# TensorE's order in an attention unit: eight value instructions as one block, both mask matmuls behind it

## The chip, the cores and the metric

The kernel runs on one core of a Trainium2 chip. Its time is the device time in microseconds (us) of one launch. PE is TensorE's matmul row in the profile and PEld its weight loads, DVE is VectorE, ACT is ScalarE, POOL is GpSimd, and SP is the engine that issues the DMAs.

## The reference, cut to what matters

32 batches of x with 256 rows and 128 columns pass an attention of 16 heads of width 64 and then a feed-forward part whose operands are quantized to FP4. The part of the attention that this change is about:

```python
s = jnp.einsum('bhid,bhjd->bhij', q * scale, k)
gm = jax.lax.stop_gradient(jnp.max(s, axis=-1, keepdims=True))
causal_mask = jnp.triu(jnp.ones((N, N), bool), 1)
p = jnp.where(causal_mask, 0.0, jnp.exp(s - gm))
num = jnp.einsum('bhij,bhjd->bhid', p, v)
out = num / (jnp.sum(p, axis=-1, keepdims=True) + EPS)
out = out.transpose(0, 2, 1, 3).reshape(B, N, H * Dh)
return out @ Wo + bo
```

The maximum `gm` is taken over all scores, the masked ones too. So the kernel must read the whole bank for the maximum first, and may put the mask on it only after that.

## The kernel before, in words

A batch is cut into eight units (0 to 7) of two heads each. The engines run the same loop over the batches, each with its own order written out by hand, and semaphores tie them together. The attention of a unit is a pipeline over several units. In unit u, TensorE does in this order:

- the first place, (u, "a"): always a `qk` step, the projection of q and k of the unit two further on into one of two PSUM banks `ps_m` (L825, three matmuls on `wq_r`, three on `wkv_r`);
- the scores of head 0 (L908, four matmuls into `ps_s`);
- the second place, (u, "b"): a step of another part, such as `gate` (units 1 and 2), `wo` (unit 3, the output projection of the batch before, L863) or `v`;
- the scores of head 1 (L908). They go to a bank that both units use, so they wait for the exponentials of unit u-1 (`exp_done`);
- the transposes of the probabilities of unit u-2 (L804, `ps_t`);
- the third place, (u, "c"): `v` in units 0 and 3, `up` in 1 and 2, `xt` in 4, `hqt` in 5, `down` in 6, none in 7;
- `mask(u, 0)` (L917, one bf16 matmul that adds a large negative number to the diagonal blocks of head 0's bank);
- the value product of unit u-3 (L960, 64 output columns for each head): two instructions for the first 128 keys, then `mask(u, 1)`, then two for the last 128 keys. The profile shows each of these fp32 instructions as two records, eight in all for a unit.

The steps in the places take the two `ps_m` banks in turn, and each first waits until the step before it in its bank has been read. In units 0 to 5 the third place has the bank that the first place of the same unit filled. So it waits for `qk_ready`, which DVE signals when it has subtracted the rounded part (L664), and DVE can do that only behind ACT's cast (L547).

ACT's order in a unit: the cast of the first place's `qk` (L547), its reads for the second place, the copies of the transposes (L570, L572), its reads for the third place, four exponentials (L583: two for each head; each head waits for its own mask through `masked`), and the copy of the value product out of PSUM (L590, which signals `ot_ready`). DVE's order: the maximum of head 0 (L774), the subtraction L664, the maximum of head 1, the reciprocals of the sums (L788, L791), and then its other parts. POOL multiplies the probabilities by the reciprocals (L454, L456) and rounds for the FP4 parts. `wo` in unit 3 waits for `ot_ready` of the last unit of its batch, which ACT signals at the end of unit 2.

Of the kernel before, what the change touches and what calls it, by code (L numbers as in the profile page):

```python
# [13 lines left out]
P = 128  # L14
# [70 lines left out]
def adaln_block(nc, x, w_q, w_kv, w_o, b_o, w_gate, w_up, w_down, cond, w_mod, out):  # L85
# [14 lines left out]
    with ExitStack() as ctx:  # L100
# [95 lines left out]
        def scores_bank(u, h):  # L196

            return u % 2 if h == 0 else 2
# [101 lines left out]
        def i_is(i, n):  # L300

            return isinstance(i, int) and i == n

        def iterations(eng, body, last=B - 1):

            for i in range(-1, 3):
                body(i)
            with eng.Fori(3, last) as i:
                body(i)
            for i in range(last, B + 2):  # L310
                body(i)
# [17 lines left out]
        def shared_steps(i):  # L329

            steps = []
            for at in ([i - 1] if not isinstance(i, int) or i > -1 else []) + [i]:
                for n, place in enumerate(sorted(PLACES)):
                    kind, behind, part = PLACES[place]
                    if i_is(at, 1) and place in WEIGHT_PLACES:
                        steps.append((at is i, place, "weights", 0, WEIGHT_PLACES.index(place), n % 2))
                    elif not isinstance(at, int) or 0 <= at - behind < B:
                        steps.append((at is i, place, kind, at - behind, part, n % 2))
            found = {}
            for n, (now, place, kind, b, part, bank) in enumerate(steps):  # L340
                if now:
                    same = [x for x in steps[:n] if x[5] == bank]
                    found[place] = (kind, b, part, bank, same[-1][2:5] if same else None)
            return found
# [457 lines left out]
        def _(pe):  # L802
            def transpose(dst, src, n=P):
                return nc.tensor.transpose(dst, src, ident[0:n, 0:n])  # L804
# [87 lines left out]
            def body(i):  # L892
                has = Has(i)
                shared = shared_steps(i)

                def at_place(u, place):
                    if (u, place) in shared:
                        kind, b, k, bank, before = shared[u, place]
                        if before is not None:

                            ready, per_batch = READ[before[0]]
                            pe.wait_ge(ready, per_batch * before[1] + (before[2] + 1) * per_batch // PARTS[before[0]])
                        shared_step(kind, b, k, bank)

                def scores(u, h):
                    for t in range(2):
                        for part in range(2):
                            mm = nc.tensor.matmul(ps_s[:, scores_bank(u, h), t * N:(t + 1) * N],  # L908
                                                  stack[:, u % 4, h, 0, t * P:(t + 1) * P], stack[:, u % 4, h, 2 - part, :],
                                                  start=(t == 0 and part == 0), stop=(part == 1), skip_group_check=True)  # L910
                    mm.then_inc(s_full, 1)

                def mask(u, h):

                    pe.wait_ge(max_ready, 16 * i + 2 * u + h + 1)
                    diagonals = ps_s[:, scores_bank(u, h), :].rearrange("p (n j) -> p n j", j=P)[:, 0:4:3, :]
                    nc.tensor.matmul(diagonals, ident_b[:, :], later_b[:, :].unsqueeze(1).to_broadcast([P, 2, P]),  # L917
                                     start=False, stop=True, skip_group_check=True).then_inc(masked, 1)

                for u in range(UNITS):  # L920
                    par = u % 2
                    at_place(u, "a")

                    if has.attn:
                        pe.wait_ge(stacked[par], STACKED * i + UNIT_STACKED * (u // 2 + 1))
                        scores(u, 0)
                    at_place(u, "b")
                    if has.attn:
                        if has.after(u - 1):
                            pe.wait_ge(exp_done, 16 * i + 2 * (u - 1) + 2)  # L930
                        scores(u, 1)
                    if i_is(i, 0) and u == 2:
                        pe.wait_ge(setup_dve, SETUP_ROWS)
                    if has.unit(u - 2):

                        g = (u - 2) % UNITS
                        for h in range(2):
                            pe.wait_ge(probs_ready, 16 * i + 2 * (u - 2) + h + 1)
                            if has.after(u - 3):
                                pe.wait_ge(pt1_ready if h else pt0_ready, UNITS * i + u - 2)  # L940
                            for c in range(3):
                                mm = transpose(ps_t[:, h, c * P:(c + 1) * P], probs[:, g % 4, h, c * P:(c + 1) * P])
                            mm.then_inc(pt_full, 1)
                    at_place(u, "c")
                    if has.attn:
                        mask(u, 0)
                    if has.unit(u - 3):

                        w = (u - 3) % UNITS
                        pe.wait_ge(pt0_ready, UNITS * i + u - 2)  # L950
                        pe.wait_ge(pt1_ready, UNITS * i + u - 2)
                        if u >= 3:
                            pe.wait_ge(v_ready, 4 * i + (4 if w >= UNITS // 2 else 2))
                        if has.after(u - 4):
                            pe.wait_ge(ot_ready, UNITS * i + u - 3)
                    for n, (keys, q0) in enumerate(((0, 0), (1, P))):
                        if has.unit(u - 3):
                            for h in range(2):
                                head = (2 * w + h) * DH
                                mm = nc.tensor.matmul(ps_o[h * DH:(h + 1) * DH, q0:N], v[:, keys, head:head + DH],  # L960
                                                      probs_t[:, w % 2, h, (0 if n == 0 else N):(N if n == 0 else 3 * P)],
                                                      start=(n == 0), stop=(n == 1), skip_group_check=True)
                        if n == 0 and has.attn:
                            mask(u, 1)
                    if has.unit(u - 3):
                        mm.then_inc(o_full, 1)

            iterations(pe, body)


# [19 lines left out]
```

## Time and profile before

| what | before |
|---|---|
| median of 3 runs | 1419.08 us (1416.86 to 1421.19) |
| span of the profiled execution | 1416.3 us |
| granted TensorE clock, mean | 0.981 of full speed |
| PE, DVE, ACT, POOL busy | 96%, 81%, 68%, 61% |
| chain that ended last | PE 46%, POOL 27%, issue 13%, DVE 9% |
| mask L917, PE | 512 matmuls, 143.6 us |
| value product L960, PE | 2048 records, 278.8 us |

The profiled execution took 1416.3 us from its first to its last instruction, 2.8 us under the median of the runs. PE's busy time overlaps itself, since its matmuls are pipelined and their ends are modelled. So lengths on PE are best read from the start of one group to the start of the next. A row of the timeline stands for a group of the same instructions in a row, with its start, its length and the count.

### The profile page before, as it was taken

To read this page: it belongs to the slowest core of one execution; us is meant where nothing else is said; L and a number is where in the kernel's file an instruction comes from. 1 tells how busy PE (TensorE), PEld (TensorE's weight loads), DVE (VectorE), ACT (ScalarE), POOL (GpSimd) and SP (SyncE) were. 2 spreads that over 40 slices of the span, in tenths; PEclk is the share of its full clock that TensorE was granted. 3 is DMA by queue.
4 is the path that set the end of the run, shared out by engine and by line. 5 is a ranking of instruction groups with operands and counts; after the bars stand their busy time and mean duration, and the time that the engine had idled before them with its cause. 6 is when DMAs were issued, how large, how long until landed. Compare 5 with 4: busy or idle time off the path is not lost.

```text
span 1416.3 us, 37184 instructions
## 1 busy us (share of the span) xinstructions
PE 1361.8 (96%) x10194; PEld 1077.6 (76%) x10194; DVE 1146.0 (81%) x2821; ACT 964.8 (68%) x3269; POOL 868.4 (61%) x1582
## 2 busy tenths in 40 slices
PE   4899999999999999999999999999999999999993
PEld 3677787778777787877778777777877787787772
DVE  5668888888888888888888888888888888888774
ACT  2767667667767667767767767766776767676750
POOL 0556666766666666656666566666666666665663
PEclk6999999999999999999999999999999999999995
DMA  5766777767677676677767667776667776667740
GB/s 153 184 164 161 163 173 175 170 161 162 161 169 179 165 166 162 160 169 177 167 165 164 159 161 176 174 167 161 162 161 169 179 167 164 162 161 169 167 97 10
DMA packets 160941, 227.99 MB, mean 161 GB/s; under 512 B 27376, under 2 KB 90736, under 8 KB 160912
## 3 DMA queue, kind: packets, MB, share of 16 engines
q1 hardware_dynamic: 160912, 227.65, 68.3%
q8 instruction: 13, 0.21, 0.1%
q14 instruction: 16, 0.13, 0.0%
HBM read 21.94 MB, written 4.28 MB: 19 GB/s over the span
## 4 chain that ended last, share of the span: by engine, by line
PE 46%; POOL 27%; issue 13%; DVE 9%; SPq 2%; DMA 1%; POOLq 1%; ACT 1%; DVEq 0%; ACTq 0%
PE ps_m L825 15%; POOL probs L456 10%; PE ps_o L960 9%; PE ps_s L908 8%; PE ps_t L804 6%; POOL qy L74 4%; POOL qy L72 4%; POOL hq L76 3%; PE ps_m L888 3%; PE ps_s L917 3%; DVE neg_max L774 2%; POOL rstd L464 1%; POOL h L492 1%; POOL h2a L488 1%; POOL probs L454 1%
## 5 line engine op out<-in xcount | busy, mean ns | idle before, releaser
L774 DVE TENSOR_REDUCE neg_max<-ps_s 128x2 f32<-128x512 f32 x512 | 351.4, 687 | 170.6 <-PE ps_s L908 165.2
L583 ACT ACTIVATE probs<-ps_s,neg_max 128x128 f32<-128x128 f32 (+1 forms) x1024 | 419.2, 427 | 39.5 <-PE ps_s L917 36.4
L456 POOL TENSOR_SCALAR probs<-probs,r_den 128x256 f32<-128x256 f32 (+1 forms) x768 | 380.3, 511 | 0.0
L454 POOL TENSOR_TENSOR probs<-probs,r_den 128x128 f32<-128x128 f32 x256 | 102.7, 401 | 427.0 <-DVE r_den L791 422.2
L908 PE MATMUL ps_s<-stack 128*128 128x256 f32 x2048 | 329.6, 287 | 3.5 <-DMA stack<-qk_parts 3.2
L908 PEld LDWEIGHTS ps_s<-stack 128*128 128x128 f32 x2048 | 285.3, 190 | 10.9 <-DMA stack<-qk_parts 4.4
L960 PE MATMUL ps_o<-probs_t,v 128*64 128x256 f32 (+1 forms) x2048 | 278.8, 351 | 0.0
L804 PE MATMUL ps_t<-ident,probs 128*128 128x128 f32 x1536 | 220.2, 275 | 4.1 <-POOL probs L456 0.4
L583 ACT ACTIVATION_READ_ACCUMULATOR probs<-ps_s,neg_max 128x1 f32 x1024 | 216.3, 211 | 0.0
L570 ACT COPY probs_t<-ps_t 128x384 f32<-128x384 f32 x160 | 77.0, 481 | 192.1 <-PE ps_t L804 192.1
L804 PEld LDWEIGHTS ps_t<-ident,probs 128*128 128x128 f32 x1536 | 172.8, 140 | 16.2 <-POOL probs L456 11.9
L664 DVE TENSOR_TENSOR qk_parts<-ps_m,qk_parts 128x512 fp32r<-128x512 f32 x256 | 174.2, 680 | 4.9 <-ACT qk_parts L547 4.9
L572 ACT COPY probs_t<-ps_t 128x384 f32<-128x384 f32 x256 | 123.8, 483 | 76.6 <-PE ps_t L804 76.5
L547 ACT CAST qk_parts<-ps_m 128x512 fp32r<-128x512 f32 x256 | 154.7, 604 | 17.4 <-PE ps_m L825 5.4
L825 PE MATMUL ps_m<-h_r,wq_r 128*128 128x256 f32 x768 | 159.6, 316 | 5.1 <-DVE h_r L599 1.6
L960 PEld LDWEIGHTS ps_o<-probs_t,v 128*64 128x64 f32 x2048 | 101.5, 134 | 73.5 <-issue 27.6
L825 PEld LDWEIGHTS ps_m<-h_r,wq_r 128*128 128x128 f32 x768 | 107.9, 190 | 50.8 <-issue 45.3
L917 PE MATMUL ps_s<-later_b,ident_b 128*128 128x256 bf16 x512 | 143.6, 281 | 2.5 <-DVE neg_max L774 2.2
L917 PEld LDWEIGHTS ps_s<-later_b,ident_b 128*128 128x128 bf16 x512 | 49.2, 96 | 126.6 <-issue 93.7
L825 PE MATMUL ps_m<-h_r,wkv_r 128*128 128x256 f32 x768 | 135.2, 285 | 0.0
L825 PE MATMUL ps_m<-wkv_r,h_r 128*128 128x512 f32 x384 | 117.6, 415 | 5.1 <-DVE qk_parts L664 4.2
L863 PE MATMUL ps_m<-wo,o_t 128*128 128x128 f32 x1024 | 119.5, 275 | 0.6 <-DVE hh L688 0.6
(109 smaller groups left out, 2018.4 us busy)
## 6 DMA issues: line engine op xcount, KB each, us to landing
stack<-qk_parts SPq DMA_DIRECT2D x512, 192.0 KB, 2.7
stack<-qk_parts SPq DMA_DIRECT2D x512, 128.0 KB, 2.7
stack<-qk_parts SPq DMA_DIRECT2D x512, 64.0 KB, 2.3
mod_a<-mod_rows SPq DMA_DIRECT2D x32, 256.0 KB, 4.0
x_in<-L_attn_x SPq DMA_DIRECT2D x32, 128.0 KB, 2.1
x_res<-L_attn_x SPq DMA_DIRECT2D x32, 128.0 KB, 2.1
out<-y_out SPq DMA_DIRECT2D x32, 128.0 KB, 1.9
mod_b<-mod_rows SPq DMA_DIRECT2D x32, 64.0 KB, 2.8
```

Source lines behind the costliest of these rows:

```text
L456: ins = nc.gpsimd.tensor_scalar(cols, cols, r_den[:, par, s:s + 1], 1.0, ALU.mult, ALU.mult)
L547: nc.scalar.copy(qk_parts[:, k % 2, :, 0, :], ps_m[bank][:, :].rearrange("p (n j) -> p n j", n=2)).then_inc(qk_high, 1)
L572: nc.scalar.copy(probs_t[:, u % 2, 1, :], ps_t[:, 1, 0:3 * P]).then_inc(pt1_ready, 1)
L583: ins = nc.scalar.activation(probs[:, u % 4, h, t * P:(1 + 2 * t) * P], ps_s[:, scores_bank(u, h), t * N:t * N + (1 + t) * P], ACT.Exp, bi ...
L664: nc.vector.tensor_tensor(qk_parts[:, k % 2, :, 1, :], ps_m[bank][:, :].rearrange("p (n j) -> p n j", n=2), qk_parts[:, k % 2, :, 0, :], A ...
L774: nc.vector.tensor_reduce(neg_max[:, par, 2 * h:2 * h + 2], ps_s[:, scores_bank(u, h), :].rearrange("p (t j) -> p t j", t=2), AX.X, ALU.ma ...
L804: return nc.tensor.transpose(dst, src, ident[0:n, 0:n])
L825: mm = nc.tensor.matmul(dst, left[l], right[r], start=(n == 0), stop=(n == 2))
L863: mm = nc.tensor.matmul(ps_m[bank][:, t * P:(t + 1) * P], o_t[:, u, t * P:(t + 1) * P], wo[:, u, :], start=(u == 0), stop=(u == UNITS - 1))
L908: mm = nc.tensor.matmul(ps_s[:, scores_bank(u, h), t * N:(t + 1) * N], stack[:, u % 4, h, 0, t * P:(t + 1) * P], stack[:, u % 4, h, 2 - pa ...
L917: nc.tensor.matmul(diagonals, ident_b[:, :], later_b[:, :].unsqueeze(1).to_broadcast([P, 2, P]), start=False, stop=True, skip_group_check= ...
L960: mm = nc.tensor.matmul(ps_o[h * DH:(h + 1) * DH, q0:N], v[:, keys, head:head + DH], probs_t[:, w % 2, h, (0 if n == 0 else N):(N if n == ...
```

## The change

Only TensorE's program changes. The value product of unit u-3 is issued as one block of four instructions (eight records) right behind the third place, and both masks of unit u follow the block.

```diff
                     at_place(u, "c")
-                    if has.attn:
-                        mask(u, 0)
                     if has.unit(u - 3):
...
-                    for n, (keys, q0) in enumerate(((0, 0), (1, P))):
-                        if has.unit(u - 3):
+                        for n, (keys, q0) in enumerate(((0, 0), (1, P))):
                             for h in range(2):
...
-                        if n == 0 and has.attn:
-                            mask(u, 1)
-                    if has.unit(u - 3):
                         mm.then_inc(o_full, 1)
+                    if has.attn:
+                        mask(u, 0)
+                        mask(u, 1)
```

The value product's line number becomes L957. The programs of ACT and DVE are the same, and so are those of POOL and SP, which the diff does not touch.

The first place is TensorE's row in unit 1 of a batch in the middle of the run, from the third place (`up`) to the first place of unit 2. Before:

```order
L825 MATMUL ps_m<-wgu_r,xq_r 128x352 [waits qk_ready]
L825 MATMUL ps_m<-wgu_r,xq_r 128x352 x2
L915 REGISTER_ALU
L917 MATMUL ps_s<-later_b,ident_b 128x2x128 [waits max_ready]
L960 MATMUL ps_o<-probs_t,v 64x256 [waits ot_ready,pt1_ready,pt0_ready]
L960 MATMUL ps_o<-probs_t,v 64x256
L915 REGISTER_ALU
L917 MATMUL ps_s<-later_b,ident_b 128x2x128 [waits max_ready]
L960 MATMUL ps_o<-probs_t,v 64x128 x2
L902 REGISTER_ALU
L825 MATMUL ps_m<-h_r,wq_r 128x256 [waits gated]
```

And now:

```order
L825 MATMUL ps_m<-wgu_r,xq_r 128x352 [waits qk_ready]
L825 MATMUL ps_m<-wgu_r,xq_r 128x352 x2
L957 MATMUL ps_o<-probs_t,v 64x256 [waits ot_ready,pt1_ready,pt0_ready]
L957 MATMUL ps_o<-probs_t,v 64x256
L957 MATMUL ps_o<-probs_t,v 64x128 x2
L915 REGISTER_ALU
L917 MATMUL ps_s<-later_b,ident_b 128x2x128 [waits max_ready]
L915 REGISTER_ALU
L917 MATMUL ps_s<-later_b,ident_b 128x2x128 [waits max_ready]
L902 REGISTER_ALU
L825 MATMUL ps_m<-h_r,wq_r 128x256 [waits gated]
```

The first mask has moved behind four value instructions, and the second follows it at once; the value instructions for the first and the last keys stand together.

The second place is TensorE's row from the end of unit 2 to the output projection `wo` in unit 3. Before:

```order
L960 MATMUL ps_o<-probs_t,v 64x256
L915 REGISTER_ALU
L917 MATMUL ps_s<-later_b,ident_b 128x2x128 [waits max_ready]
L960 MATMUL ps_o<-probs_t,v 64x128 x2
L825 MATMUL ps_m<-h_r,wq_r 128x256 [waits gated]
L825 MATMUL ps_m<-h_r,wq_r 128x256 x2
L825 MATMUL ps_m<-h_r,wkv_r 128x256 x3
L908 MATMUL ps_s<-stack 128x256 [waits stacked1]
L908 MATMUL ps_s<-stack 128x256 x3
L863 MATMUL ps_m<-wo,o_t 128x128 [waits ot_ready,h_ready]
L863 MATMUL ps_m<-wo,o_t 128x128 x15
L908 MATMUL ps_s<-stack 128x256 [waits exp_done]
```

And now:

```order
L915 REGISTER_ALU
L917 MATMUL ps_s<-later_b,ident_b 128x2x128 [waits max_ready]
L915 REGISTER_ALU
L917 MATMUL ps_s<-later_b,ident_b 128x2x128 [waits max_ready]
L825 MATMUL ps_m<-h_r,wq_r 128x256 [waits gated]
L825 MATMUL ps_m<-h_r,wq_r 128x256 x2
L825 MATMUL ps_m<-h_r,wkv_r 128x256 x3
L908 MATMUL ps_s<-stack 128x256 [waits stacked1]
L908 MATMUL ps_s<-stack 128x256 x3
L863 MATMUL ps_m<-wo,o_t 128x128 [waits ot_ready,h_ready]
L863 MATMUL ps_m<-wo,o_t 128x128 x15
L908 MATMUL ps_s<-stack 128x256 [waits exp_done]
```

The last mask of unit 2 now stands directly ahead of the `qk` step, with no value instructions between them; between the masks and the `wo` step, which waits for `ot_ready`, stand that step and four score matmuls, as before. (`REGISTER_ALU` rows compute the thresholds of waits.)

## Rows read from the trace of the kernel before

**Rows 1.** The page, busy time of each engine (us, share of the span, instructions)
```profile
PE 1361.8 (96%) x10194; PEld 1077.6 (76%) x10194; DVE 1146.0 (81%) x2821; ACT 964.8 (68%) x3269; POOL 868.4 (61%) x1582
```
**Rows 2.** The page, engines' shares of the chain that ended last
```profile
PE 46%; POOL 27%; issue 13%; DVE 9%; SPq 2%; DMA 1%; POOLq 1%; ACT 1%; DVEq 0%; ACTq 0%
```
**Rows 3.** Timeline of PE, one batch: start us, length us, engine, line, operation, xcount
```profile
699.77 0.97 PE L825 MATMUL ps_m<-wkv_r,h_r 128*128 128x512 f32 x3
700.58 0.28 PE L917 MATMUL ps_s<-later_b,ident_b 128*128 128x256 bf16 x1
...
704.80 0.75 PE L825 MATMUL ps_m<-wgu_r,xq_r 128*128 128x352 f32 x3
705.39 0.28 PE L917 MATMUL ps_s<-later_b,ident_b 128*128 128x256 bf16 x1
705.61 0.65 PE L960 MATMUL ps_o<-probs_t,v 128*64 128x256 f32 x4
...
706.77 0.61 PE L825 MATMUL ps_m<-h_r,wq_r 128*128 128x256 f32 x3
...
711.57 0.61 PE L825 MATMUL ps_m<-h_r,wq_r 128*128 128x256 f32 x3
...
712.86 3.73 PE L863 MATMUL ps_m<-wo,o_t 128*128 128x128 f32 x32
...
717.49 0.95 PE L825 MATMUL ps_m<-wkv_r,h_r 128*128 128x512 f32 x3
...
722.77 0.38 PE L804 MATMUL ps_m<-ident,xn 128*128 128x128 f32 x2
722.99 0.27 PE L917 MATMUL ps_s<-later_b,ident_b 128*128 128x256 bf16 x1
...
727.25 0.50 PE L804 MATMUL ps_m<-ident,hq 128*128 128x128 f32 x3
727.59 0.27 PE L917 MATMUL ps_s<-later_b,ident_b 128*128 128x256 bf16 x1
...
731.82 1.50 PE L888 MATMUL ps_m<-wd_t,hq_t 128*128 128x128 f32 x12
733.16 0.27 PE L917 MATMUL ps_s<-later_b,ident_b 128*128 128x256 bf16 x1
...
734.53 0.61 PE L825 MATMUL ps_m<-h_r,wq_r 128*128 128x256 f32 x3
...
737.66 0.27 PE L917 MATMUL ps_s<-later_b,ident_b 128*128 128x256 bf16 x1
...
741.86 0.97 PE L825 MATMUL ps_m<-wkv_r,h_r 128*128 128x512 f32 x3
```
**Rows 4.** Timeline of ACT in the same batch; in brackets the idle time before it
```profile
701.26 0.37 ACT L583 ACTIVATE probs<-ps_s,neg_max 128x128 f32<-128x128 f32 x1
...
702.86 0.39 ACT L590 COPY o_t<-ps_o 128x256 f32<-128x256 f32 x1
703.11 0.63 ACT L547 CAST qk_parts<-ps_m 128x512 fp32r<-128x512 f32 x1
...
733.47 0.37 ACT L583 ACTIVATE probs<-ps_s,neg_max 128x128 f32<-128x128 f32 x1 [0.97 <-PE ps_s L917]
```
**Rows 5.** Timeline of DVE in unit 1 of that batch
```profile
703.46 0.69 DVE L774 TENSOR_REDUCE neg_max<-ps_s 128x2 f32<-128x512 f32 x1 [1.16 <-PE ps_s L908]
704.07 0.68 DVE L664 TENSOR_TENSOR qk_parts<-ps_m,qk_parts 128x512 fp32r<-128x512 f32 x1
```
**Rows 6.** Timeline near the start, ACT and DVE, where the subtraction waits for the cast
```profile
22.08 0.59 ACT L547 CAST qk_parts<-ps_m 128x512 fp32r<-128x512 f32 x1 [2.53 <-PE ps_m L825]
...
22.70 0.69 DVE L664 TENSOR_TENSOR qk_parts<-ps_m,qk_parts 128x512 fp32r<-128x512 f32 x1 [2.36 <-ACT qk_parts L547]
```
**Rows 7.** Timeline of PE near the end: all value instructions of a unit, no mask
```profile
1372.73 0.87 PE L960 MATMUL ps_o<-probs_t,v 128*64 128x256 f32 x8
1373.53 1.23 PE L825 MATMUL ps_m<-wgu_r,xq_r 128*128 128x352 f32 x6
```

## The prediction

> **What bounds the kernel now.** I read three things in this order. First the page's busy times: PE is at 96% of the span, DVE at 81%, ACT at 68% [rows 1]. The chain that ended last is PE for only 46%, and POOL has 27% of it [rows 2], so PE's 96% isn't a proof that PE sets the time. Second, PE's timeline over one batch in steady state, because only the start-to-start distances show what PE can issue: from the third place of unit 0 to the same place of the next batch it takes 741.86 - 699.77 = 42.09 us [rows 3], and 32 batches of that are 1347 of the 1416 us. PE's rows hardly leave a gap. Third, and this decides, the timelines of ACT and DVE beside it: what does each third place on PE wait for, and with how much to spare?
>
> In unit 1 the third place starts at 704.80 [rows 3]. It waits for DVE's subtraction, which started at 704.07 [rows 5], so the way from the start of the subtraction to the place is 0.73 us. The subtraction started behind the maximum of head 0 (703.46, 0.69 long) and not behind ACT's cast, which ended at 703.11 + 0.63 = 703.74 [rows 4, 5]. So ACT's cast is early by about 0.3 us. What sets the cast is ACT's own row: four exponentials from 701.26, the copy of the value product at 702.86, the cast at 703.11 [rows 4]. That row cannot start before mask 0.
>
> This gives a loop that closes in every unit whose third place waits for the subtraction: first exponential E, cast, subtraction, third place, mask 0, next E. Now mask 0 comes directly behind the third place, and the loop has slack. The change puts the whole value block into it.
>
> **What the change takes off PE.** Before, from the first mask to the next first place: 706.77 - 705.39 = 1.38 us [rows 3]. The same eight value records without a mask among them take 1373.53 - 1372.73 = 0.80 [rows 7]. A mask takes 705.61 - 705.39 = 0.22 ahead of value instructions; three 512-column matmuls take 700.58 - 699.77 = 0.81, at most 0.135 for each 256 columns [rows 3], so some 0.09 of the 0.22 is the passage to the 64-column instructions. My estimate for the new stretch: 0.09 to get into the block, 0.80 for it, 0.11 for each mask = 1.11, which is 0.27 less than 1.38. Bounds: the passage costs 0 to 0.10; the block costs 0.80 to 0.95 (the latter is 1.38 less two masks of 0.22, as if the two halves saved nothing together). If PE alone set the time, this would be 256 units x 0.27 = 69 us of gain.
>
> The Trainium skill, "TensorEngine Tiling (Array Packing)", section Key Properties, says that changing the tiling mode, not just the tile, drains the engine. The rows agree as far as they go: the 0.22 against 0.135, and 0.80 against 0.95. By that rule the change has two mode changes a unit where before had four, and one of the two now stands ahead of E.
>
> **What it adds to the loop.** E now comes at the third place's own length T, plus 0.09, plus 0.80, plus the way from mask 0 to the exponential where ACT is free, 733.47 - 733.16 = 0.31 [rows 3, 4]. Together T + 1.20. From E on: four exponentials 702.86 - 701.26 = 1.60; the copy 703.11 - 702.86 = 0.25 [rows 4]; cast to subtraction 22.70 - 22.08 = 0.62 where DVE really waited for it [rows 6], which I take as 0.66 because that cast was 0.59 long and the one behind the copy is 0.63; subtraction to third place 0.73. Sum 3.24. The loop is then 4.44 + T. Nothing hides it: ACT's row and DVE's subtraction are in series with PE. The maximum of head 0, now early, doesn't bind any more.
>
> Now unit by unit, E to E [all T from rows 3]:
> - unit 0 (`v`): T = 0.81, so 5.25.
> - units 1 and 2 (`up`): T = 705.39 - 704.80 = 0.59, so 5.03 each, 10.06.
> - unit 3: here PE has more than 4 us of `wo`, so the loop over the subtraction is loose. But `wo` waits for the copy of the last unit's value product, on ACT behind the exponentials of unit 2. The copy ends at E + 1.60 + 0.39 = 1.99 [rows 4]; with 0.06 for the semaphore (a subtraction's end at 704.07 + 0.68 lies 0.05 ahead of the place that waits for it) `wo` starts at 2.05. PE would be there sooner: masks end 0.09 before E (0.22 less 0.31), and from the first place to `wo` it is 712.86 - 711.57 = 1.29, so at 1.20. The 0.85 us that PE had ahead are lost in front of `wo`. From `wo` to the third place 717.49 - 712.86 = 4.63, then 0.81 (a `v`) + 1.20: 8.69.
> - unit 4 (`xt`): T = 722.99 - 722.77 = 0.22, so 4.66. Unit 5 (`hqt`): T = 727.59 - 727.25 = 0.34, so 4.78.
> - unit 6 (`down`): its third place is not tied to its own first place; it comes 731.82 - 727.25 = 4.57 behind that of unit 5, held by DVE and POOL work that starts with unit 5's subtraction. I keep that. T = 733.16 - 731.82 = 1.34. E to E: 4.57 + 1.34 - 0.34 = 5.57.
> - unit 7 (no third place): PE alone. From the first place to mask 0 737.66 - 734.53 = 3.13, plus 1.20, less 0.09: 4.24.
>
> Sum: 5.25 + 10.06 + 8.69 + 4.66 + 4.78 + 5.57 + 4.24 = 43.25 us a batch against 42.09, so 1.16 more; x 32 = 37 us. The profiled execution would go from 1416.3 to about 1453, and the median, which stands 2.8 us above it, from 1419.1 to **1456 us**, 2.6% slower.
>
> Edits with little effect: both masks wait for maxima that DVE has done by then (head 1's maximum ends about 0.6 us behind the start of the third place, and both masks come over 1 us behind it); the value block's own waits (copies of unit u-3, its PSUM bank) were over a unit ago. Queued behind a late third place on PE are the value block, the masks, then everything of the next unit; who waits for these is ACT. SP's DMAs start from the same subtractions, a little later each batch, but so do their readers.
>
> **Rivals.**
> First, **PE sets the time and the gain is real**: 69 us, so 1350 us. For it: 96% busy and no visible gaps. The Trainium skill, "Perfetto Trace Analysis", section Identifying the Most-Contended Engine, says that the engine with the highest occupancy is the one to optimize, but also that TensorE's matmul busy share is a poor measure. By the first half alone this rival would be the forecast. The point from which it decides: the loop must be shorter than PE's own unit. From the third place of unit 0 to that of unit 1 it is 704.80 - 699.77 = 5.03 now [rows 3], so 4.76 for PE alone afterwards, and the loop is 0.81 + 4.44 = 5.25. Against it speaks that sum of measured rows, which would have to be 0.5 us too long in each unit. 6%.
>
> Second, **`wo` isn't held**: the copy is in time and unit 3 keeps its 0.85 us. Then 32 x 0.85 = 27 us less, 1429 us. Against it: the program waits for `ot_ready` ahead of the first of the `wo` matmuls, and ACT's copy stands behind the exponentials. 6%. With the passage into the block at 0 as well (seven units x 0.09 x 32 = 20 us) it ends near 1409; I count that as 2% on the faster side.
>
> Third, **the block saves nothing when it's whole**: 0.95 for 0.80, in seven units of eight at least, 7 x 0.15 x 32 = 34 us more, 1490 us. Against it: rows 7. 5%.
>
> Fourth, **the masks' delay is hidden** by other slack that I took for closed, such as a cast that starts ahead of the copy's end, so that losses and gains cancel: 1415 to 1423. 5%.
>
> **The numbers.** The forecast has 76%; its own range is 1438 to 1475, from 0.62 to 0.69 for cast to subtraction (7 us), 0 to 0.10 for the passage (20 us) and the masks' way to E. The range that I give is 1427 to 1485; it takes in the second rival. About 0.3% is what a measurement here can tell from no change. Faster: 6 + 2 = 8%; within 0.3%: 5%; slower: 76 + 6 + 5 = 87%.
>
> **What would show it.** Right: PE's start-to-start from the third place of unit 1 to that of unit 2 goes to about 5.0; gaps on PE of 0.3 us or more ahead of the third places, put down to DVE's subtraction; DVE's idle time ahead of the subtraction put down to ACT's cast; a gap of about 0.8 ahead of `wo`, put down to ACT's copy L590; the eight value records as one group with 0.80 to the mask. PE's share falls below 93%. Wrong: a batch under 42 us, subtractions that still start right behind the maximum of head 0, or a `wo` with no wait.

## The result and the profile after

The changed kernel takes 1475.11 us (median of 4 runs, 1474.16 to 1475.84) against 1418.86 us for the kernel before: ratio 1.0393, 95% interval 1.0379 to 1.0408. It is 56 us slower. The prediction said slower, 1456 us, range 1427 to 1485; 1475 is the upper end of the narrower range, 1438 to 1475, that it gave for its own mechanism.

First the page of the changed kernel: busy time with share of the span, the chain that ended last by engine and by line, and four groups with their idle time and what ended it.

```profile
PE 1353.1 (92%) x10194; PEld 1087.8 (74%) x10194; DVE 1150.4 (78%) x2821; ACT 961.0 (65%) x3269; POOL 868.0 (59%) x1582
...
PE 51%; ACT 27%; DVE 9%; issue 9%; SPq 2%; DMA 1%; POOL 1%; ACTq 0%; DVEq 0%; POOLq 0%
ACT probs L583 18%; PE ps_o L957 13%; PE ps_m L825 10%; PE ps_m L863 8%; DVE qk_parts L664 7%; ACT qk_parts L547 5%; PE ps_s L908 5%; PE ps_s L917 4%; PE ps_t L804 4%; PE ps_m L888 3%; ACT o_t L590 3%; PE ps_m L804 2%; DMA stack<-qk_parts 1%; DMA wkv<-L_attn_Wkv 1%; SPq L395 0%
...
L583 ACT ACTIVATE probs<-ps_s,neg_max 128x128 f32<-128x128 f32 (+1 forms) x1024 | 417.6, 420 | 215.7 <-PE ps_s L917 215.7
...
L908 PEld LDWEIGHTS ps_s<-stack 128*128 128x128 f32 x2048 | 278.9, 190 | 88.9 <-ACT probs L583 82.9
L664 DVE TENSOR_TENSOR qk_parts<-ps_m,qk_parts 128x512 fp32r<-128x512 f32 x256 | 176.2, 688 | 83.9 <-ACT qk_parts L547 83.9
...
L863 PE MATMUL ps_m<-wo,o_t 128*128 128x128 f32 x1024 | 121.9, 277 | 26.9 <-ACT o_t L590 26.3
```

PE's share went from 96% to 92% [rows 1], and ACT, which was hardly in the chain before [rows 2], now has 27% of it; its largest line is the exponential. Three waits that were small have become regular: the scores of head 1 wait for the exponentials, DVE's subtraction waits for ACT's cast (in the trace 186 times out of 256), and the output projection waits for ACT's copy of the value product.

Now PE's timeline over one batch of the changed kernel.

```profile
704.97 0.39 PE L917 MATMUL ps_s<-later_b,ident_b 128*128 128x256 bf16 x2
...
728.01 0.97 PE L825 MATMUL ps_m<-wkv_r,h_r 128*128 128x512 f32 x3
728.91 0.87 PE L957 MATMUL ps_o<-probs_t,v 128*64 128x256 f32 x8
729.72 0.39 PE L917 MATMUL ps_s<-later_b,ident_b 128*128 128x256 bf16 x2
729.86 0.60 PE L825 MATMUL ps_m<-h_r,wq_r 128*128 128x256 f32 x3
...
733.36 0.75 PE L825 MATMUL ps_m<-wgu_r,xq_r 128*128 128x352 f32 x3
734.04 0.87 PE L957 MATMUL ps_o<-probs_t,v 128*64 128x256 f32 x8
734.84 0.39 PE L917 MATMUL ps_s<-later_b,ident_b 128*128 128x256 bf16 x2
734.99 0.60 PE L825 MATMUL ps_m<-h_r,wq_r 128*128 128x256 f32 x3
...
738.50 0.75 PE L825 MATMUL ps_m<-wgu_r,xq_r 128*128 128x352 f32 x3
...
739.98 0.39 PE L917 MATMUL ps_s<-later_b,ident_b 128*128 128x256 bf16 x2
...
740.93 0.63 PE L908 MATMUL ps_s<-stack 128*128 128x256 f32 x4
742.43 3.81 PE L863 MATMUL ps_m<-wo,o_t 128*128 128x128 f32 x32 [0.87 <-ACT o_t L590]
...
747.13 0.95 PE L825 MATMUL ps_m<-wkv_r,h_r 128*128 128x512 f32 x3
748.00 0.87 PE L957 MATMUL ps_o<-probs_t,v 128*64 128x256 f32 x8
748.81 0.39 PE L917 MATMUL ps_s<-later_b,ident_b 128*128 128x256 bf16 x2
```

The value block is as forecast: 729.72 - 728.91 = 0.81, 734.84 - 734.04 = 0.80 [rows 7]. The pair of masks is shorter than forecast: from the first of them to the next first place 729.86 - 729.72 = 0.14, where I had 0.22. From the start of the third place to the next first place it takes 734.99 - 733.36 = 1.63 in unit 1, where before it took 706.77 - 704.80 = 1.97 [rows 3]. So PE has 0.34 less to do in a unit, and not 0.27. Yet a batch, from mask to mask in unit 3, takes 748.81 - 704.97 = 43.84 us, against 42.09 before; 32 x 1.75 = 56 us.

ACT and DVE in the same batch show the loop that closes (unit 0's exponential, unit 1's cast and subtraction, then the exponentials of units 1 and 2, and the copy that releases `wo`):

```profile
730.11 0.37 ACT L583 ACTIVATE probs<-ps_s,neg_max 128x128 f32<-128x128 f32 x1 [0.51 <-PE ps_s L917]
...
731.72 0.38 ACT L590 COPY o_t<-ps_o 128x256 f32<-128x256 f32 x1
731.97 0.62 ACT L547 CAST qk_parts<-ps_m 128x512 fp32r<-128x512 f32 x1
...
735.24 0.37 ACT L583 ACTIVATE probs<-ps_s,neg_max 128x128 f32<-128x128 f32 x1 [1.39 <-PE ps_s L917]
...
740.30 0.37 ACT L583 ACTIVATE probs<-ps_s,neg_max 128x128 f32<-128x128 f32 x1 [1.32 <-PE ps_s L917]
...
741.90 0.38 ACT L590 COPY o_t<-ps_o 128x256 f32<-128x256 f32 x1
```

```profile
731.33 0.69 DVE L774 TENSOR_REDUCE neg_max<-ps_s 128x2 f32<-128x512 f32 x1 [0.78 <-PE ps_s L908]
732.62 0.69 DVE L664 TENSOR_TENSOR qk_parts<-ps_m,qk_parts 128x512 fp32r<-128x512 f32 x1 [0.59 <-ACT qk_parts L547]
```

Read it with PE's rows: exponential 730.11, copy 731.72, cast 731.97, subtraction 732.62 (after 0.59 us of idle time that the cast ended, where before it started right behind the maximum [rows 5]), third place 733.36, value block 734.04, masks 734.84, exponential 735.24. Each step starts when the one before it releases it. At the third place TensorE's weight load tells what it waited for:

```profile
733.36 0.46 PEld L825 LDWEIGHTS ps_m<-wgu_r,xq_r 128*128 128x128 f32 x3 [0.32 <-DVE qk_parts L664]
```

From first exponential to first exponential (the starts of L583 in each trace; u is the unit at whose exponential the stretch ends):

| unit | before | forecast | after | mask 0, block, mask 1 (e2) |
|---|---|---|---|---|
| 0 | 5.12 | 5.25 | 5.35 | 4.78 |
| 1 | 4.53 | 5.03 | 5.13 | 4.25 |
| 2 | 4.72 | 5.03 | 5.06 | 4.54 |
| 3 | 8.44 | 8.69 | 8.83 | 8.50 |
| 4 | 4.86 | 4.66 | 4.82 | 4.58 |
| 5 | 4.38 | 4.78 | 4.85 | 4.66 |
| 6 | 5.28 | 5.57 | 5.56 | 4.94 |
| 7 | 4.76 | 4.24 | 4.24 | 4.41 |
| batch | 42.09 | 43.25 | 43.84 | 40.67 |

Units 6 and 7 come out as forecast, but they close by another way. From the exponential of unit 5 on, ACT and TensorE's weight loads show:

```profile
714.97 0.37 ACT L583 ACTIVATE probs<-ps_s,neg_max 128x128 f32<-128x128 f32 x1 [0.54 <-PE ps_s L917]
716.74 0.53 PEld L908 LDWEIGHTS ps_s<-stack 128*128 128x128 f32 x4 [0.61 <-ACT probs L583]
...
720.53 0.37 ACT L583 ACTIVATE probs<-ps_s,neg_max 128x128 f32<-128x128 f32 x1 [1.88 <-PE ps_s L917]
...
722.30 0.54 PEld L908 LDWEIGHTS ps_s<-stack 128*128 128x128 f32 x4 [0.26 <-ACT probs L583]
...
724.76 0.37 ACT L583 ACTIVATE probs<-ps_s,neg_max 128x128 f32<-128x128 f32 x1 [0.54 <-PE ps_s L917]
```

In both units the scores of head 1 wait for the four exponentials of the unit before (1.77 us from the first of them), and from there PE's own row, with no other wait that moves it, leads to the next exponential: 1.77 + 3.79 = 5.56 and 1.77 + 2.46 = 4.23 (the table's 4.24, to rounding).

### The profile page after: what moved, and what is told of

It is laid out like the page before. It is cut to its first block, busy times and chain, and to the rows that moved or that the text cites. A ratio compares the mean times of both kernels' runs of the same rounds, so it can differ in the third digit from the quotient of the medians.

```text
span 1473.7 us, 37184 instructions
## 1 busy us (share of the span) xinstructions
PE 1353.1 (92%) x10194; PEld 1087.8 (74%) x10194; DVE 1150.4 (78%) x2821; ACT 961.0 (65%) x3269; POOL 868.0 (59%) x1582
## 4 chain that ended last, share of the span: by engine, by line
PE 51%; ACT 27%; DVE 9%; issue 9%; SPq 2%; DMA 1%; POOL 1%; ACTq 0%; DVEq 0%; POOLq 0%
ACT probs L583 18%; PE ps_o L957 13%; PE ps_m L825 10%; PE ps_m L863 8%; DVE qk_parts L664 7%; ACT qk_parts L547 5%; PE ps_s L908 5%; PE ps_s L917 4%; PE ps_t L804 4%; PE ps_m L888 3%; ACT o_t L590 3%; PE ps_m L804 2%; DMA stack<-qk_parts 1%; DMA wkv<-L_attn_Wkv 1%; SPq L395 0%
## 5 line engine op out<-in xcount | busy, mean ns | idle before, releaser
L583 ACT ACTIVATE probs<-ps_s,neg_max 128x128 f32<-128x128 f32 (+1 forms) x1024 | 417.6, 420 | 215.7 <-PE ps_s L917 215.7
L908 PE MATMUL ps_s<-stack 128*128 128x256 f32 x2048 | 352.3, 295 | 33.2 <-ACT probs L583 22.3
L908 PEld LDWEIGHTS ps_s<-stack 128*128 128x128 f32 x2048 | 278.9, 190 | 88.9 <-ACT probs L583 82.9
L957 PE MATMUL ps_o<-probs_t,v 128*64 128x256 f32 (+1 forms) x2048 | 223.4, 339 | 0.5 <-ACT o_t L590 0.5
L804 PE MATMUL ps_t<-ident,probs 128*128 128x128 f32 x1536 | 210.9, 273 | 0.6 <-POOL probs L456 0.5
L583 ACT ACTIVATION_READ_ACCUMULATOR probs<-ps_s,neg_max 128x1 f32 x1024 | 208.1, 203 | 0.0
L957 PEld LDWEIGHTS ps_o<-probs_t,v 128*64 128x64 f32 x2048 | 124.4, 136 | 95.1 <-issue 54.5
L547 ACT CAST qk_parts<-ps_m 128x512 fp32r<-128x512 f32 x256 | 158.3, 618 | 7.7 <-PE ps_m L825 5.1
L825 PE MATMUL ps_m<-h_r,wq_r 128*128 128x256 f32 x768 | 156.0, 312 | 4.7 <-DVE h_r L599 2.2
L863 PEld LDWEIGHTS ps_m<-wo,o_t 128*128 128x128 f32 x1024 | 116.7, 192 | 32.5 <-issue 31.7
L825 PEld LDWEIGHTS ps_m<-h_r,wkv_r 128*128 128x128 f32 x768 | 110.3, 191 | 0.0
```

What stands on the lines that cost most here:

```text
L547: nc.scalar.copy(qk_parts[:, k % 2, :, 0, :], ps_m[bank][:, :].rearrange("p (n j) -> p n j", n=2)).then_inc(qk_high, 1)
L583: ins = nc.scalar.activation(probs[:, u % 4, h, t * P:(1 + 2 * t) * P], ps_s[:, scores_bank(u, h), t * N:t * N + (1 + t) * P], ACT.Exp, bi ...
L825: mm = nc.tensor.matmul(dst, left[l], right[r], start=(n == 0), stop=(n == 2))
L863: mm = nc.tensor.matmul(ps_m[bank][:, t * P:(t + 1) * P], o_t[:, u, t * P:(t + 1) * P], wo[:, u, :], start=(u == 0), stop=(u == UNITS - 1))
```

## The experiments

Eight kernels, each timed in three rounds against the kernel before on the same chip; its median there was 1419.7 us for e1, e2, e4 and e5 and 1420.5 for the others. In the diffs `m0`, `m1` are the masks, `v0`, `v1` the halves of the value product, `v` the whole; each line is the order behind the third place.

| kernel | median us | ratio to before, 95% interval |
|---|---|---|
| changed: v, m0, m1 | 1475.1 | 1.0393 (1.0379 to 1.0408) |
| e1: m0, m1, v | 1391.3 | 0.9802 (0.9786 to 0.9819) |
| e2: m0, v, m1 | 1378.1 | 0.9706 (0.9689 to 0.9722) |
| e3: v0, m0, m1, v1 | 1444.0 | 1.0171 (1.0154 to 1.0188) |
| e4: changed, ACT's copy behind the cast | 1452.6 | 1.0233 (1.0216 to 1.0250) |
| e5: changed, `wo` waits late | 1440.8 | 1.0153 (1.0136 to 1.0170) |
| e6: changed order in units 5 and 6 alone | 1415.6 | 0.9965 (0.9953 to 0.9978) |
| e7: e2 with `wo`'s late wait | 1371.9 | 0.9654 (0.9638 to 0.9670) |
| e8: e4 and e5 together | 1411.5 | 0.9937 (0.9920 to 0.9953) |

### Is it the late mask or the merged block? e1 and e2

```diff
# e1
-v, m0, m1
+m0, m1, v
# e2
-v, m0, m1
+m0, v, m1
```

> Order: both masks right behind the third place, then the eight value records as one block. It keeps the whole saving on TensorE (1.38 to about 1.11 us a unit) and takes the value block out of the loop exponential, cast, subtraction, third place. Theory (the delay of mask 0 costs, the merged block saves): faster than before, by 0.9 to 1.3 us a batch, so 1375 to 1392 us; the second mask waits some 0.2 us for head 1's maximum in units 4, 5 and 7, and DVE and POOL hold units 3 to 6 partly. Rival (the merged block itself is what costs, whichever side of the masks it is on): slower than before, near 1475.

> Order: mask 0, the eight value records as one block, mask 1. TensorE saves the same as in the changed kernel, mask 0 is where it was before, and mask 1 comes about 0.2 us later than ACT could take it. Theory: faster than before, 1375 to 1395 us, within 0.5% of the kernel with both masks first. Rival (merged block costs): near 1475. Rival (the loop counts with the last exponential, so mask 1 matters as much as mask 0): 1419 or more.

Both keep the merged block, and both beat the kernel before, e2 by 42 us in its own rounds. So the block is a gain, and the rival that it costs is out. PE's timeline of e2 in unit 1:

```profile
729.11 0.75 PE L825 MATMUL ps_m<-wgu_r,xq_r 128*128 128x352 f32 x3
729.70 0.28 PE L917 MATMUL ps_s<-later_b,ident_b 128*128 128x256 bf16 x1
729.91 0.87 PE L962 MATMUL ps_o<-probs_t,v 128*64 128x256 f32 x8
730.71 0.28 PE L917 MATMUL ps_s<-later_b,ident_b 128*128 128x256 bf16 x1
730.75 0.60 PE L825 MATMUL ps_m<-h_r,wq_r 128*128 128x256 f32 x3
```

Mask 0 comes at 0.59 behind the third place, as before [rows 3], and the whole stretch from the mask to the next first place is 730.75 - 729.70 = 1.05, against 1.38. e2 and the changed kernel give PE the same instructions; only mask 0's place differs, and that is worth 1475 - 1378 = 97 us. The 56 us of the result are therefore some 41 us gained by the merged block and 97 us lost by the late mask. e2's rival, that mask 1 matters as much, is out too.

e1 is 13 us slower than e2. In its table of waits (engine, line, waited for, us in total, times, longest) of one batch stands

```profile
PEld ps_s L917 <- DVE neg_max L774: 1.3, 4, 0.4
```

where e2 has 0.3 us in one wait (and the kernel before 0.7 in two): mask 1 directly behind mask 0 comes before DVE has the maximum of head 1. From exponential to exponential, units 7 and 0 of e1 take 4.83 and 5.08, where e2 has 4.41 and 4.78, and unit 3 takes 8.28 for 8.50. That comes to 0.5 us a batch or 16 us, close to the 13. Which part of it is the masks' wait was not tried by itself.

### How much of the delay counts? e3

```diff
-v, m0, m1
+v0, m0, m1, v1
```

> Order: the first half of the value block (first 128 keys), both masks, the second half. Mask 0 is late by the first half alone, 0.58 us instead of 0.80. TensorE's stretch grows from 1.11 to 1.26 us a unit, since the block is cut. Theory (what stands between the third place and mask 0 counts one for one in the loop): 0.22 less in each of seven units, 0.15 more in unit 7, 1.4 us a batch less than the changed kernel: about 1435 us, between 1428 and 1445. Rival (TensorE's own work sets the time): slower than the changed kernel by 8 x 0.15 x 32 = 38 us, 1510.

```profile
717.10 0.75 PE L825 MATMUL ps_m<-wgu_r,xq_r 128*128 128x352 f32 x3
717.78 0.65 PE L962 MATMUL ps_o<-probs_t,v 128*64 128x256 f32 x4
718.36 0.39 PE L917 MATMUL ps_s<-later_b,ident_b 128*128 128x256 bf16 x2
718.68 0.44 PE L962 MATMUL ps_o<-probs_t,v 128*64 128x128 f32 x4
719.05 0.62 PE L825 MATMUL ps_m<-h_r,wq_r 128*128 128x256 f32 x3
```

The mask is 718.36 - 717.78 = 0.58 behind the block's start, 0.22 earlier than in the changed kernel. The kernel is 31 us faster than the changed one, though PE has more to do. The batch went from 43.84 to 42.86. The theory said about 40 us (1.4 a batch); the sign is as it said, and the rival (some 38 us slower) is out. From exponential to exponential, units 0, 1, 2, 3 and 5 lose 0.22 to 0.23 each, which is one for one. The shortfall of 0.4 lies in three units. Unit 6 loses 0.02 (5.54 after 5.56), where I had 0.22. Unit 7, which PE alone sets here, takes 4.50 after 4.24, where I had 4.39: the row from the block's start to the next first place is 719.05 - 717.78 = 1.27, where the changed kernel has 0.95, so the cut costs 0.32 and not 0.15. Unit 4 loses 0.12.

### Shortening the loop elsewhere: e4, e5, e8

```diff
# e4, ACT's program
-four exponentials; copy o_t (L590); next unit: cast qk (L547)
+four exponentials; next unit: cast qk; copy o_t
# e5, TensorE's wo step
-wait ot_ready 8(b+1); 16 matmuls
+wait ot_ready 8(b+1)-1; 14 matmuls (units 0 to 6 of the batch)
+wait ot_ready 8(b+1); 2 matmuls (unit 7)
```

> The changed kernel, with ACT's copy of the value product (L590) moved behind the next unit's cast. It takes 0.25 us out of the loop between the exponentials and the third place in units 0, 1, 2, 4 and 5, and holds the output projection by the length of the cast more (about 0.5 us) in unit 3. Theory: 5 x 0.25 less 0.5 = 0.75 us a batch, 24 us less than the changed kernel: about 1451 us. Rival (the loop over ACT isn't what sets the time, TensorE's own order is): within 5 us of 1475, or slower by the later projection, 1490.

> The changed kernel, with the output projection's wait for the last unit's value product moved behind the 14 of its 16 matmuls that do not need it. Theory: the gap of 0.87 us in front of it in every batch goes, and nothing else is late behind it: 32 x 0.87 = 28 us less than the changed kernel, 1447 us. Rival (DVE's continuous work from unit 2 to unit 4 holds the third place there): only a part, 1460 to 1475.

> The changed kernel with both single edits together: ACT's copy behind the next cast (23 us alone), and the projection's late wait (35 us alone). With the wait out of the way the later copy costs nothing in unit 3, so it should be worth its full 5 x 0.25 x 32 = 40 us. Theory: 1475 - 35 - 40 = 1400 us, between 1393 and 1412, better than the kernel before. Rival (TensorE or DVE binds by then): no less than 1418.

ACT's timeline of e4:

```profile
704.48 0.37 ACT L586 ACTIVATE probs<-ps_s,neg_max 128x128 f32<-128x128 f32 x1 [0.48 <-PE ps_s L917]
...
706.08 0.60 ACT L547 CAST qk_parts<-ps_m 128x512 fp32r<-128x512 f32 x1
706.54 0.41 ACT L568 COPY o_t<-ps_o 128x256 f32<-128x256 f32 x1
```

The cast starts 1.60 behind the exponential instead of 731.97 - 730.11 = 1.86, and the copy (now 0.41 long) ends at 2.47 instead of 1.98. 22.5 us less than the changed kernel, forecast 24: nothing on TensorE was touched, so ACT's row is in the loop. By unit, from exponential to exponential, it is 0.27 to 0.28 less in units 0, 1, 2 and 4, 0.48 more in unit 3, and 0.07 less in unit 5, where I had 0.25. Units 6 and 7 stay at 5.57 and 4.23: ACT's cast isn't on their way.

PE's timeline of e5 around `wo` (now on other lines):

```profile
721.70 0.64 PE L912 MATMUL ps_s<-stack 128*128 128x256 f32 x4
722.18 3.73 PE L866 MATMUL ps_m<-wo,o_t 128*128 128x128 f32 x32
725.66 0.72 PE L912 MATMUL ps_s<-stack 128*128 128x256 f32 x4
```

The gap is gone: `wo` starts 722.18 - 721.70 = 0.48 behind the scores, where in the changed kernel it was 742.43 - 740.93 = 1.50. That is 1.02 a batch, 33 us; measured 34. I had 28, since I took the idle time that the profile prints (0.87). That time is counted from the modelled end of the scores and not from their issue.

e8 has both and ends at 1411.5, inside the forecast range and 9 us under the kernel before, with the masks still late. The two edits take 64 us off together, where they take 22.5 and 34.3 alone. That the later copy is worth 29 us with `wo` out of the way and not 40 has a place. The stretch of unit 5 stays at 4.86; by the trace POOL's probabilities hold the transposes there (a wait of 0.3 us). Unit 4 loses 0.15, and units 0, 1 and 2 lose 0.26 to 0.28 each.

### Where a late mask is free: e6

```diff
-all units: m0, v0, m1, v1
+units 5 and 6: v, m0, m1; the others: m0, v0, m1, v1
```

> The changed order in units 5 and 6 alone, the order of before in the other six. The masks of unit u lead to the third place of unit u+1; those of units 6 and 7 do not wait for a cast that follows these masks (unit 6's waits for an earlier step, unit 7 has none). Theory: late masks cost nothing there and TensorE saves up to 0.27 in unit 6, and less in unit 5, since POOL holds unit 6: 1408 to 1414 us. Rival (late masks cost alike in every unit): two eighths of +56 us, 1433.

```profile
733.01 0.87 PE L962 MATMUL ps_o<-probs_t,v 128*64 128x256 f32 x8
733.82 0.39 PE L917 MATMUL ps_s<-later_b,ident_b 128*128 128x256 bf16 x2
733.96 0.60 PE L825 MATMUL ps_m<-h_r,wq_r 128*128 128x256 f32 x3
...
737.15 0.27 PE L917 MATMUL ps_s<-later_b,ident_b 128*128 128x256 bf16 x1
```

5 us less than the kernel before; the interval (0.9953 to 0.9978) lies below 1 and far from the rival's 1433. Unit 6 has its masks late, at 733.82, but unit 7's mask follows 737.15 - 733.82 = 3.33 later, against 737.66 - 733.16 = 4.50 before [rows 3]: the delay is made good within one unit. From exponential to exponential, units 5 and 6 take 0.62 and 0.29 more than before, and unit 7 takes 1.17 less. 1415.6 lies just above the 1408 to 1414 that I had expected. So the price of a late mask depends on who waits for its exponentials, not on the mask.

### A better version: e7

```diff
-v, m0, m1
+m0, v, m1
-wait ot_ready 8(b+1); 16 matmuls
+wait ot_ready 8(b+1)-1; 14 matmuls
+wait ot_ready 8(b+1); 2 matmuls
```

> Mask 0, the value block, mask 1, and the output projection's wait moved behind 14 of its 16 matmuls. In the kernel with mask 0, block, mask 1 TensorE still stood some 0.3 us in front of the projection in each batch. Theory: up to 0.3 x 32 = 10 us less, 1368 to 1374 us. Rival (DVE's continuous work from unit 2 to unit 4 holds the third place): the same 1378 us within 3.

1371.87 us, 3.5% under the kernel before and the best of all. The gap before `wo` was 0.3 us in e2, and closing it gave 6.3 us, as expected. Unit 3 became 0.40 shorter, and unit 4 took half of that back (4.78 after 4.58).

## Why the prediction was right, and where its size was off

- **The bound.** Right: PE's 96% didn't mean that PE alone sets the time. With TensorE's instructions unchanged in number, ACT's program alone moved the time by 22 us (e4), and mask 0's place by 97 us (e2 against the changed kernel).
- **What comes off PE.** Right in kind: 0.80 for the block, and the stretch shorter. The masks were mis-sized: 0.14 for the two, where I had 0.22, so the saving is 0.34 a unit and not 0.27. PE alone would then have given 256 x 0.34 = 87 us and not 69. The result doesn't show this error, since PE waits in the changed kernel. In e2 the full 0.34 is seen in units 0, 6 and 7 (4.78, 4.94 and 4.41 against 5.12, 5.28 and 4.76), and e2 is 42 us faster. No order reached more than 49: in e2, unit 5 takes longer than before (4.66 against 4.38), though PE has less to do in it, and in one batch of e2 the transposes' weight loads wait 1.0 us for POOL's probabilities, where before it was 0.4. That DVE and POOL keep the rest is my reading and was not tried. (The upper bound of 0.95 for the block was also 0.01 off: 1.38 less two masks of 0.22 is 0.94.)
- **The loop.** From the exponential to the third place 733.36 - 730.11 = 3.25, forecast 3.24. Third place to block 0.68 (0.59 + 0.09), block 0.80, as forecast. That a part counts one for one was tried on two of them: the time ahead of mask 0 (e3, where it held in units 0 to 3 and 5) and ACT's copy (e4, where it held in units 0, 1, 2 and 4). DVE's part was not tried.
- **Unit 3.** Right in kind: `wo` waits for ACT's copy, and e5 takes the wait away for 34 us. The size was 0.14 short: `wo` starts 742.43 - 740.30 = 2.13 behind the exponential (I had 2.05) and takes 4.70 (4.63) to the third place; the way from there to the block is 0.03 shorter. The copy ends at 742.28 as forecast, but `wo` follows it by 0.15 and not by 0.06.
- **Units 6 and 7.** 5.56 and 4.24, forecast 5.57 and 4.24, but that is luck: both had the wrong way. I had unit 6 held by work of DVE and POOL, and unit 7 by PE alone. In the trace both wait for the exponentials at the scores of head 1, a wait that the forecast doesn't have. In unit 7 the shorter masks bring PE's row forward by 0.08, and that wait takes about the same back.
- **The terms that were mis-sized.** The batch is 43.84 - 43.25 = 0.59 over the forecast: 19 us, all of the difference between 1456 and 1475. No single term has it. The way from mask 0 to the exponential gives 0.18: I took 0.31 from unit 6 for all units, and in units 0 and 1 it is 735.24 - 734.84 = 0.40 (in unit 2 it is 740.30 - 739.98 = 0.32). Unit 3 gives 0.14, unit 4 0.16 and unit 5 0.07. The third places of these last two are transposes, which start a little later behind the subtraction and take longer ahead of the block: 0.37 and 0.47 where I had 0.31 and 0.43. The remaining 0.04 are spread over units 0, 1, 2 and 6. The first of these terms stood in the trace of before: mask 0 of unit 1 at 705.39 [rows 3] has its exponential 0.40 later, though ACT was free.

```profile
705.79 0.37 ACT L583 ACTIVATE probs<-ps_s,neg_max 128x128 f32<-128x128 f32 x1 [0.18 <-PE ps_s L917]
```

- **What would show it.** All came, one of them in part. (The third places of units 1 and 2 stand 738.50 - 733.36 = 5.14 apart, where I had about 5.0.) As forecast, the gap ahead of the third place is 0.3 us, but in unit 1 nearly as much idle time stands one step earlier, at the scores of head 1, which wait for the exponentials (82.9 us in the page for all units). The forecast doesn't have that wait. In units 0 to 2, 4 and 5 it isn't the last one, since behind it and the transposes PE waits again for DVE; in units 6 and 7 it is.

By the rule that I quoted from the Trainium skill, "TensorEngine Tiling (Array Packing)", section Key Properties, a change of tiling mode drains the engine. The trace after fits that rule: an `up` step takes 0.68 to the block and 0.59 to a mask, so one change costs 0.09. Whether the engine drains in that time no row shows.

## What to carry to other kernels

An engine at 96% can have the end of a loop over other engines right behind it. Before moving an instruction later in a busy engine's row, add up the loop that starts with its result (who waits for it, what they release, and when this engine waits for that) and compare it with the engine's own length; here the spare was 0.3 us and the delay 0.9. Put every wait on the way into the sum, also one that isn't the last today: in units 6 and 7 such a wait, at the scores of head 1, came to set the pace. Grouping like instructions did pay, as long as the one that others wait for stayed in front: mask 0, block, mask 1 gave 2.9%, and a wait moved behind the work that doesn't need it gave the rest of 3.5%.

## What the runs showed of the hardware that I had not expected

With ACT idle, the exponential follows its mask by 0.40 us in units 0 and 1 of the changed kernel and by 0.32 us in the others; before, unit 1 had 0.40 and units 2 and 6 had 0.32 and 0.31. It is the same in each of 24 batches in the middle of either trace, to 0.002 us. The instructions are the same in all units. The cause was not tried and stays open.
